# A two-layer graph kernel on one core: node passes one after the other, earlier stores of gathered rows, ten source-row buffers, and message arithmetic column by column on ScalarE

## The chip, the cores and the metric

The kernel runs on one core of a Trainium2 chip. The metric is device time in microseconds (us) of one execution; lower is better. The core has TensorE (PE: matmuls; PEld: its weight loads), VectorE (DVE), ScalarE (ACT), GpSimd (POOL), and SyncE (SP), which here only issues DMAs. POOL issues all indirect DMAs: gathers and scatters of one row for each of 128 partitions.

## The reference, cut to what matters

There are 100,000 nodes with 64 features, and 50,000 edges (src, dst), sorted by dst.

```python
h = relu(layernorm(x))
x = x + gcn(h)            # two GCN layers, 64 -> 128 -> 64, on all nodes
h = relu(layernorm(x))
x = x + l1(h)             # relation attention over the edges
# gcn layer: deg = count(dst) + 1; dinv = rsqrt(deg)
#   agg[dst] += h[src] * dinv[src] * dinv[dst];  out = agg + h * dinv^2 + b
# l1: att = sum(t_r * tanh(h_r + efeat)); a = softmax of att over the edges of one dst
#   h_nb[dst] += h[src] * a
#   out = leaky((h + h_nb) @ res_w1.T) + leaky(h * h_nb @ res_w2.T)
```

A node that is no destination has no sum over edges, so it needs only dense arithmetic. A destination is worked out again at its last edge, and its row is scattered over the dense result.

## The kernel before, in words

Nodes are held in NB = 49 blocks of 2048 (128 partitions x CB = 16 nodes). Edges are held as KE = 392 columns of 128; GE = 28 groups of GT = 14 columns. The program is written out by hand, engine by engine, with a semaphore for each hand-over. In order of time its stages are these.

- **Counting.** `hot(t)` makes two one-hot tiles in 16 bit for each of the 392 edge columns on VectorE: `lo_hot` (128 wide, L454) and `hi_hot` (784 wide, L455), four buffers each. TensorE multiplies them (L1534) and so adds up the degree of every node. Meanwhile POOL gathers x of each destination into `own` (5 buffers of a group); SP stores each group to the table `xd_t` in `keep_own`.
- **T pass** (`step_t`, 49 blocks): load x, layer norm and relu, store a row of 64 features plus a place and 1/sqrt(degree) to `node_rows`.
- **Q pass** (`step_q`, 49 blocks): load those rows and x, run the dense GCN (L1553, L1559, L1560, L1567), store `g1_t`; second layer norm, store `h_t`; residual products (L1575, L1583), store the output. `over_nodes` mixes the two passes: after step 5 one `step_q` follows every second `step_t`, on every engine, and the rest of `step_q` comes last. On SP, `own_after(turn)` says after which turn a gathered `own` group is stored: group g at turn 8 + 7g/4, none earlier.
- **E pass** (28 edge groups): once all T rows are stored, POOL gathers the rows of the sources into `near` (NBR = 6 buffers of a group, in the memory of the T pass); group g waits until VectorE has used group g - NBR (`S["d1"]`, L638). VectorE scales, runs a segmented scan (L641) and normalizes. It starts when all of the Q pass is stored.
- **D pass** (28 groups), the permutation by relation, the relation products and the softmax follow. The change touches there only the names of semaphores.
- **F pass** (28 groups, `step_f` on VectorE). For each group: message = neighbour row times weight (L912), scan (L916), sum of weights and its reciprocal (L920, L921), quotient into `fnb` (L922), the two operands of the product (L926, L927), then for the first segment of each partition mask, reduce and add (L929 to L931); then `f_post` of the group before (leaky L562, L900, and L902, which writes `fout`, two buffers, once the scatters of two groups before have landed). ScalarE copies between TensorE's banks (L1501, L1507) and spreads the mask (L1495). POOL scatters 14 columns of each finished group (L1196).

L1201 and L1196 are the helpers of all gathers and scatters, and L977 that of SP's DMAs, so their rows are told apart by the names of the tiles.

Of the kernel before, what the change touches and what calls it, by code (L numbers as in the profile page):

```python
# [5 lines left out]
ALU = mybir.AluOpType  # L6
ACT = mybir.ActivationFunctionType
AX = mybir.AxisListType
# [4 lines left out]
P = 128  # L13
# [48 lines left out]
NBR = 6  # L62
# [30 lines left out]
def build(nc, x, src, dst, eattr, etype, w1, b1, w2, b2, relw, rw1, rw2, out):  # L93
    with ExitStack() as ctx:
# [102 lines left out]
        near = part(arena, 0, [NBR, GT, TW])  # L197
# [4 lines left out]
        lo_hot = part(arena, Q0 + KN // 2, [4, P], F16)  # L202
        hi_hot = part(arena, Q0 + KN // 2 + 2 * P, [4, KN], F16)
        H0 = Q0 + KN // 2 + 2 * P + 2 * KN
# [35 lines left out]
        own = part(work, 0, [OWN, GW])  # L240
        W0 = OWN * GW
# [25 lines left out]
        fmask = part(work, 4 * FW, [DW * GT])  # L267
# [45 lines left out]
        lo_key, hi_key = m_idx[:].bitcast(F32), pos  # L313
        hot_made, hot_used = sem("one_hots_made"), sem("one_hots_used")
# [4 lines left out]
        Q = sems("q", "steps turned at h relu u g1 added x1 centered square var std hn hturned ht o os out")  # L319
# [8 lines left out]
        G = sems("d", "steps d1 mat run x1 centered square var std h")  # L328
# [10 lines left out]
        f = sems("f", "steps mat run two turned t o os half out")  # L339
# [39 lines left out]
        def _(dve):  # L379
# [26 lines left out]
            o.did(v.tensor_copy(lo_key[:], tmp_a[:, 0:KE].bitcast(I32)))  # L406
# [50 lines left out]
            for t in range(KE):  # L457
                hot(t)
# [38 lines left out]
            ot, oq = Steps(dve, T["steps"]), Steps(dve, Q["steps"])  # L497
# [40 lines left out]
            def q_centre(b):  # L538
# [5 lines left out]
                tt(cols(qxc), cols(x1), wide(st[:, 1, :], CB), ALU.subtract).then_inc(Q["centered"], 1)  # L544

            def q_variance(b):
                st = q_stat[:, b % 2]
                dve.wait_ge(Q["square"], b + 1)
                oq.do(v.tensor_reduce(st[:, 0, :], cols(qsq), AX.X, ALU.add))
                ts(st[:, 2, :], st[:, 0, :], 1.0 / D, EPS, ALU.mult, ALU.add).then_inc(Q["var"], 1)  # L550

            def q_h_rows(b):
                st = q_stat[:, b % 2]
                dve.wait_ge(Q["std"], b + 1)
# [1189 lines left out]
```

## Time and profile before

| what | value |
|---|---|
| time, median of 3 runs | 4637.77 us (4633.24 to 4641.26) |
| the profiled execution, its own time | 4642.34 us |
| its span, first to last instruction | 4640.6 us |
| busy | PE 34%, PEld 24%, DVE 54%, ACT 22%, POOL 65% |
| mean granted TensorE clock | 0.628 of full |
| HBM traffic | 265.55 MB read, 264.24 MB written, 114 GB/s |

No engine is busy for the whole span, and each stage has a limit of its own, so the shares are to be read stage by stage. A row of the timeline begins with the start and the duration; in brackets stands how long the engine had been idle and what released it.

### The profile page before, as it was taken

How to read it: one execution, taken by the hardware profiler on the slowest of the kernel's cores; microseconds unless marked ns; L12 is line 12 of the kernel's file. 1: busy time of each engine (PE TensorE's matmuls, PEld its weight loads, DVE VectorE, ACT ScalarE, POOL GpSimd, SP SyncE). 2: the span in 40 equal slices, each digit the busy share in tenths (PEclk: the TensorE clock that was granted, in tenths of full speed). 3: DMA queues.
4: the chain of work that ended last, by engine and by line, in shares of the span. 5: the costliest groups of instructions: out<-in, count | busy, mean ns of one | idle time of the engine just before them, and what ended most of it. 6: DMA issues, size and time to landing. Idle time of an engine off the chain costs nothing.

```text
span 4640.6 us, 31267 instructions
## 1 busy us (share of the span) xinstructions
PE 1563.3 (34%) x8094; PEld 1135.9 (24%) x8094; DVE 2526.9 (54%) x4033; ACT 1012.3 (22%) x1596; POOL 3032.0 (65%) x2761
## 2 busy tenths in 40 slices
PE   8835445688654340000000000023346600333331
PEld 2224334467543230000000000012335500322231
DVE  9967777777797666987741111112222200666663
ACT  0023333455432221111110000012222200222221
POOL 6026566640187776777757777777747777588887
PEclk9966666788776665555555555555556655666665
DMA  1056676776443334555532222234433300111110
GB/s 41 1 165 208 214 222 211 217 215 192 149 119 102 83 90 140 188 186 197 198 88 73 73 73 77 75 113 120 128 110 93 88 17 1 34 62 54 54 54 27
DMA packets 362638, 527.97 MB, mean 114 GB/s; under 512 B 220064, under 2 KB 232458, under 8 KB 362470
## 3 DMA queue, kind: packets, MB, share of 16 engines
q1 hardware_dynamic: 268166, 426.25, 28.2%
q0 software_dynamic: 94304, 99.74, 9.3%
q8 instruction: 74, 1.21, 0.1%
q14 instruction: 94, 0.77, 0.1%
HBM read 265.55 MB, written 264.24 MB: 114 GB/s over the span
## 4 chain that ended last, share of the span: by engine, by line
POOL 48%; issue 16%; PE 12%; DVE 11%; DMA 8%; ACT 2%; SPq 1%; POOLq 0%; DVEq 0%; ACTq 0%
POOL arena L1201 26%; POOL result L1196 10%; POOL slot_rows L1196 8%; DMA arena<-in_x 6%; POOL relf L1201 4%; PE banks L1534 3%; PE banks L1567 2%; PE banks L1669 2%; DMA work<-slot_rows 2%; PE banks L1559 1%; DVE arena L519 1%; SPq L977 1%; PE banks L1583 1%; DVE arena L455 1%; PE banks L1657 1%
## 5 line engine op out<-in xcount | busy, mean ns | idle before, releaser
L1201 POOL DMA_INDIRECT arena<-input_and_place_by_node,src_i x392 | 481.1, 1227 | 385.0 <-DVE arena L638 265.8
L1201 POOL DMA_INDIRECT work<-in_x,dsafe x392 | 414.1, 1056 | 435.6 <-DMA x_of_destination<-work 319.2
L1196 POOL DMA_INDIRECT result<-work,outi x392 | 502.1, 1281 | 164.3 <-issue 122.7
L1201 POOL DMA_INDIRECT arena<-g_by_node_and_edge,m_idx x392 | 445.1, 1136 | 121.1 <-issue 119.2
L1196 POOL DMA_INDIRECT slot_rows<-work,dsafe x392 | 404.3, 1031 | 141.7 <-issue 119.2
L1201 POOL DMA_INDIRECT arena<-h_by_node_and_edge,m_idx x392 | 405.3, 1034 | 119.5 <-issue 119.2
L1201 POOL DMA_INDIRECT relf<-slot_scores,src_i x392 | 369.9, 944 | 155.7 <-issue 128.5
L1657 PE MATMUL banks<-ident,work 128*128 128x128 f32 x456 | 111.5, 394 | 877.4 <-DMA work<-slot_rows 876.5
L819 DVE TENSOR_TENSOR work<-work,ends 128x896 f32<-128x896 f32 x28 | 46.7, 1668 | 568.1 <-DMA work<-h_by_node_and_edge 561.5
L1657 PEld LDWEIGHTS banks<-ident,work 128*128 128x128 f32 x456 | 80.3, 203 | 893.6 <-issue 696.0
L1669 PE MATMUL banks<-work 128*128 x912 | 209.6, 402 | 165.6 <-issue 115.1
L1567 PEld LDWEIGHTS banks<-w_sb,work 128*128 128x128 f32 x1568 | 224.4, 228 | 101.4 <-issue 101.4
L1567 PE MATMUL banks<-w_sb,work 128*128 128x64 f32 x1568 | 239.0, 316 | 0.0
L1669 PEld LDWEIGHTS banks<-work 128*128 128x128 f32 x912 | 180.0, 294 | 205.3 <-issue 205.3
L1699 PE MATMUL banks<-ident,work 128*128 128x128 f32 x392 | 90.5, 387 | 365.5 <-DVE work L927 365.5
L1553 PE MATMUL banks<-ident,arena 128*128 128x128 f32 x392 | 82.1, 347 | 388.3 <-DMA arena<-in_x 387.4
L1636 PE MATMUL banks<-last_run,carry 128*128 128x64 f32 (+1 forms) x6 | 1.8, 390 | 600.4 <-DVE last_run L775 593.2
L1534 PE MATMUL banks<-arena 128*128 128x392 f16 x784 | 195.6, 339 | 7.9 <-DVE arena L455 6.1
L833 DVE TENSOR_TENSOR dsti<-banks,work 128x256 f32<-128x256 f32 x57 | 24.2, 424 | 276.5 <-PE banks L1669 276.5
L1699 PEld LDWEIGHTS banks<-ident,work 128*128 128x128 f32 x392 | 72.2, 206 | 370.9 <-DVE work L927 370.9
L455 DVE TENSOR_SCALAR arena<-arena,pos 128x784 f16<-128x784 f16 x392 | 162.5, 415 | 0.0
L1553 PEld LDWEIGHTS banks<-ident,arena 128*128 128x128 f32 x392 | 59.7, 180 | 397.3 <-DMA arena<-in_x 341.6
(315 smaller groups left out, 5117.2 us busy)
## 6 DMA issues: line engine op xcount, KB each, us to landing
arena<-in_x SPq DMA_DIRECT2D x96, 512.0 KB, 5.3
slot_rows<-work SPq DMA_DIRECT2D x48, 912.0 KB
work<-slot_rows SPq DMA_DIRECT2D x114, 384.0 KB, 3.4
input_and_place_by_node<-arena SPq DMA_DIRECT2D x49, 528.0 KB, 2.9
arena<-input_and_place_by_node SPq DMA_DIRECT2D x49, 512.0 KB
g_by_node_and_edge<-arena SPq DMA_DIRECT2D x49, 512.0 KB, 3.3
h_by_node_and_edge<-arena SPq DMA_DIRECT2D x49, 512.0 KB, 3.1
arena<-x_of_destination SPq DMA_DIRECT2D x56, 448.0 KB, 4.3
```

The lines of the kernel that those rows point to most:

```text
L455: ts(hi_hot[:, t % 4, :], iota_h, hi_key[:, t:t + 1], None, ALU.is_equal).then_inc(hot_made, 1)
L519: stt(out=trows[:, b % 2, :, 0:D], in0=cols(tx[:, b % 3]), scalar=0.0, in1=wide(st[:, 4, :], CB), op0=ALU.max, op1=ALU.mult).then_inc(T["h ...
L819: oc.did(tt(by_column(pd1)[:, 0:GT, :], cols(phd), wide(ends[:, group(g)], GT), ALU.mult))
L977: sp.dma_start(to, of).then_inc(signal, 16)
L1196: pool.indirect_dma_start(out=table[:, :], out_offset=bass.IndirectOffsetOnAxis(ap=idx, axis=0), in_=of, in_offset=None, bounds_check=boun ...
L1201: pool.indirect_dma_start(out=to, out_offset=None, in_=table[:, :], in_offset=bass.IndirectOffsetOnAxis(ap=idx, axis=0)).then_inc(signal, 16)
L1534: ins = matmul(bank(4 + k)[:, 0:KE], lo_hot[:, t % 4, :], hi_hot[:, t % 4, k * KE:(k + 1) * KE], start=t == 0, stop=t == KE - 1, skip_grou ...
L1553: ins = transpose(bank(0)[:, k * P:(k + 1) * P], qh0[:, b % 3, half + k * P:half + (k + 1) * P], ident[:])
L1567: ins = matmul(bank(4 + n % 2)[:, k * D:(k + 1) * D], qhid[:, n % 2, at:at + P], w2_sb[:], start=True, stop=True)
L1657: ins = transpose(bank(j % 2)[:, k * P:(k + 1) * P], slot_w[:, j % SB, k, D:RW], ident[:])
L1669: ins = matmul(bank(2 + j % 4)[:, at], slot_ht[:, q, at], flat[:, w], start=True, stop=True)
L1699: ins = transpose(bank(c % 2)[:, k * P:(k + 1) * P], ftwo[:, at:at + P], ident[:])
```

## The change

Five things change; the D pass, the permutation, the relation products and the softmax keep their work.

- Counting: `lo_hot` is made for 14 columns by one `tensor_tensor` in 16 bit (128 x 1792), in two buffers; `hi_hot` stays one instruction for each column.
- The two node passes are no longer mixed: 50 turns of `step_t`, then 53 of `step_q`.
- SP stores `own` groups 0 to 11 (OWN_EARLY) before it does anything for the T pass beyond its first two loads. The other 16 are stored at turns 10, 13, 17, ... 62, each after the row store and the load of its turn.
- `near` has 10 buffers; the last four lie in the memory of `own`, so POOL waits before group 6 until every `own` group is stored.
- F pass: message, quotient and mask move from VectorE to ScalarE, as 14 activations each with a scale per partition; the sum over the mask is taken by 14 products with the identity on TensorE, added up in bank 7.

```diff
-NBR = 6
+OWN_EARLY = 12
+NBR = 10
-        near = part(arena, 0, [NBR, GT, TW])
+        near = [part(arena, k * GT * TW, [GT, TW]) for k in range(6)]
+        near += [part(work, k * GT * TW, [GT, TW]) for k in range(NBR - 6)]
             for b in range(NB + 1):
                 step_t(b)
-                if b >= 5 and b % 2:
-                    step_q((b - 5) // 2)
-            for k in range((NB - 5) // 2 + 1, NB + 4):
+            for k in range(NB + 4):
                 step_q(k)
...
-            def hot(t):
-                after(dve, hot_used, t - 3)
-                ts(lo_hot[:, t % 4, :], iota_h[:, 0:P], lo_key[:, t:t + 1], None, ALU.is_equal).then_inc(hot_made, 1)
-                ts(hi_hot[:, t % 4, :], iota_h, hi_key[:, t:t + 1], None, ALU.is_equal).then_inc(hot_made, 1)
+            for g in range(GE):
+                after(dve, hot_used, (g - 1) * GT)
+                tt(lo_hot[g % 2], iota_h[:, 0:P].unsqueeze(1).to_broadcast([P, GT, P]), wide(lo_half[:, group(g)], GT, P),
+                   ALU.is_equal).then_inc(lo_made, 1)
+                for t in range(g * GT, (g + 1) * GT):
+                    after(dve, hot_used, t - 3)
+                    ts(hi_hot[:, t % 4, :], iota_h, hi_key[:, t:t + 1], None, ALU.is_equal).then_inc(hi_made, 1)
...
# step_f on VectorE: leaves L912, L922, L929 to L931; f_post(g - 1) goes ahead of the two operands
-                    of.did(tt(by_column(fd1)[:, 1:SC, 0:D], cols(arena[:, g * GW:(g + 1) * GW]), wide(weights, GT), ALU.mult))
+                    dve.wait_ge(f["weighed"], g + 1)
-                    of.do(tt(cols(fnb), by_column(run)[:, 1:SC, 0:D], wide(st[:, 1, :], GT), ALU.mult))
+                if g > 0:
+                    f_post(g - 1)
+                if g < GE:
+                    dve.wait_ge(f["nb"], g + 1)
...
# SP
-                return [g for g in range(GE) if 8 + 7 * g // 4 == turn]
+                return [g for g in range(OWN_EARLY, GE) if 10 + 7 * (g - OWN_EARLY) // 2 == turn]
+            for g in range(OWN_EARLY):
+                keep_own(g)
             over_nodes(step_t, step_q)
# POOL, source rows
             for g in range(GE):
+                if g == 6:
+                    all_landed(pool, own_kept, OWN_KEPT)
                 after(pool, S["d1"], 2 * (g - NBR + 1))
...
# ScalarE
+            def f_weigh(g):
+                after(act, f["run"], g)
+                for k in range(GT):
+                    t = g * GT + k
+                    ins = activation(by_column(fd1)[:, 1 + k, 0:D], arena[:, t * D:(t + 1) * D], ACT.Copy, scale=weight[:, t:t + 1])
+                ins.then_inc(f["weighed"], 1)
+            def f_normal(g):
+                act.wait_ge(f["share"], g + 1)
+                after(act, f["two"], 2 * g)
+                for k in range(GT):
+                    ins = activation(cols(fnb)[:, k, :], by_column(frun[:, g % 2])[:, 1 + k, 0:D], ACT.Copy,
+                                     scale=estat[:, g % 2, 1, k:k + 1])
+                ins.then_inc(f["nb"], 1)
+            def f_masked(g):
+                after(act, f["summed"], g)
+                for k in range(GT):
+                    t = g * GT + k
+                    ins = activation(fmask[:, k, :], by_column(frun[:, g % 2])[:, 1 + k, :], ACT.Copy, scale=hm[:, t:t + 1])
+                ins.then_inc(f["masked"], 1)
             f_mat(0)
+            f_weigh(0)
             for g in range(GE):
+                f_normal(g)
                 if g + 1 < GE:
                     f_mat(g + 1)
+                    f_weigh(g + 1)
                 f_turned(g, 0)
                 for c in range(4):
                     if c < 3:
                         f_turned(g, c + 1)
+                    else:
+                        f_masked(g)
                     f_rows(g, c)
# TensorE, after the residual products of a group
+                pe.wait_ge(f["masked"], g + 1)
+                for k in range(GT):
+                    ins = matmul(bank(7)[:, 0:DW], ident[:], fmask[:, k, :], start=g == 0 and k == 0, stop=False,
+                                 skip_group_check=True)
+                ins.then_inc(f["summed"], 1)
```

## Rows read from the trace of the kernel before

**Rows 1.** Windows: busy time (x instructions) by engine, PE clock, DMA share, GB/s.

```profile
20.80:219.00 198.20, 195.56 (x784) 46.25 (x784) 197.40 (x785) 0.00 (x0) 57.22 (x59) 1.00 0.06 11
...
235.20:905.00 669.80, 326.16 (x1758) 249.08 (x1759) 507.06 (x705) 242.45 (x390) 370.05 (x344) 0.67 0.67 206
905.00:1250.50 345.50, 287.45 (x1772) 228.52 (x1770) 259.62 (x325) 183.69 (x296) 71.28 (x64) 0.84 0.63 196
```

**Rows 2.** Timeline of the counting: VectorE and TensorE's loads.

```profile
121.22 0.11 PEld L1534 LDWEIGHTS banks<-arena 128*128 128x128 f16 x2 [0.38 <-DVE arena L455]
...
121.26 0.41 DVE L455 TENSOR_SCALAR arena<-arena,pos 128x784 f16<-128x784 f16 x1
121.59 0.24 DVE L454 TENSOR_SCALAR arena<-arena,m_idx 128x128 f16<-128x128 f16 x1
```

**Rows 3.** Timeline of POOL: first and last of 70 own gathers of the counting.

```profile
5.68 1.17 POOL L1201 DMA_INDIRECT work<-in_x,dsafe  x1 [2.23 <-DVE dsafe L399]
...
94.76 0.94 POOL L1201 DMA_INDIRECT work<-in_x,dsafe  x1 [0.30 <-issue]
```

**Rows 4.** Timeline of the E pass: VectorE with two tensor inputs beside POOL's gathers.

```profile
1532.27 1.69 DVE L638 TENSOR_TENSOR arena<-arena 128x896 f32<-128x896 f32 x1 [6.43 <-DMA arena<-input_and_place_by_node,src_i]
1532.35 2.32 POOL L1201 DMA_INDIRECT arena<-input_and_place_by_node,src_i  x1 [0.30 <-issue]
```

**Rows 5.** Timeline: T pass with nothing beside it, then the first Q stores.

```profile
245.81 1.21 DVE L503 TENSOR_REDUCE t_stat<-arena 128x16 f32<-128x1024 f32 x1
...
251.25 1.21 DVE L503 TENSOR_REDUCE t_stat<-arena 128x16 f32<-128x1024 f32 x1
...
267.18 0.87 SPq L977 DMA_DIRECT2D arena<-input_and_place_by_node  x1
...
289.56 0.33 SPq L977 DMA_DIRECT2D g_by_node_and_edge<-arena  x1
```

**Rows 6.** Timeline, Q pass alone: SP's g1 stores, one a block; a start of TensorE.

```profile
928.88 0.32 SPq L977 DMA_DIRECT2D g_by_node_and_edge<-arena  x1
...
999.26 0.32 SPq L977 DMA_DIRECT2D g_by_node_and_edge<-arena  x1
...
1067.58 0.32 SPq L977 DMA_DIRECT2D g_by_node_and_edge<-arena  x1
...
1068.89 1.11 PE L1553 MATMUL banks<-ident,arena 128*128 128x128 f32 x4 [3.35 <-DMA arena<-in_x]
...
1084.73 0.32 SPq L977 DMA_DIRECT2D g_by_node_and_edge<-arena  x1
...
1095.99 0.32 SPq L977 DMA_DIRECT2D g_by_node_and_edge<-arena  x1
...
1200.37 0.34 SPq L977 DMA_DIRECT2D g_by_node_and_edge<-arena  x1
```

**Rows 7.** Windows of the source-row gathers alone: POOL busy (x gathers).

```profile
1261.30:1450.00 188.70, 154.52 (x113) 0.73 0.39 113
1450.00:1741.00 291.00, 231.58 (x196) 0.65 0.32 88
```

**Rows 8.** Timeline of the F pass: a scatter with VectorE idle, VectorE's wait.

```profile
4211.79 0.98 POOL L1196 DMA_INDIRECT result<-work,outi  x1 [0.30 <-issue]
...
4216.64 1.09 DVE L902 TENSOR_TENSOR work<-work 128x896 f32<-128x896 f32 x1 [8.73 <-DMA result<-work,outi]
...
4220.48 1.99 POOL L1196 DMA_INDIRECT result<-work,outi  x1 [0.30 <-issue]
```

**Rows 9.** Groups of instructions over the whole span: F pass, and ScalarE's sizes.

```profile
L1196 POOL DMA_INDIRECT result<-work,outi x392 | 502.1, 1281 | 164.3 <-issue 122.7 <-DVE work L902 41.6
L1349 ACT ACTIVATE arena<-arena 128x1024 f32<-128x1024 f32 x49 | 51.9, 1059 | 4.5 <-DVE arena L544 4.3
L1457 ACT COPY work<-work 128x896 f32<-128x896 f32 x28 | 47.6, 1700 | 185.1 <-DVE work L825 185.1
L1442 ACT ACTIVATE estat<-estat 128x14 f32<-128x14 f32 x28 | 6.0, 214 | 82.7 <-DVE estat L732 82.7
```

More of the change, by code:

```diff
@@ L201, in build @@
         iota_h = part(arena, Q0, [KN], F16)
-        lo_hot = part(arena, Q0 + KN // 2, [4, P], F16)
-        hi_hot = part(arena, Q0 + KN // 2 + 2 * P, [4, KN], F16)
-        H0 = Q0 + KN // 2 + 2 * P + 2 * KN
+        lo_hot = [part(arena, Q0 + KN // 2 + k * GT * P // 2, [GT, P], F16) for k in range(2)]
+        hi_hot = part(arena, Q0 + KN // 2 + GT * P, [4, KN], F16)
+        lo_half = part(arena, Q0 + KN // 2 + GT * P + 2 * KN, [KE], F16)
+        H0 = Q0 + KN // 2 + GT * P + 2 * KN + KE // 2
         iota_i = part(arena, H0, [KN], I32)
@@ L266, in build @@
         frun = part(work, 2 * FW, [2, FW])
-        fmask = part(work, 4 * FW, [DW * GT])
+        fmask = part(work, 4 * FW, [GT, DW])
         F0 = 4 * FW + DW * GT
@@ L338, in build @@
         soft = sem("softmax_steps")
-        f = sems("f", "steps mat run two turned t o os half out")
+        f = sems("f", "steps mat weighed run share nb two masked summed turned t o os half out")
         f_in, f_sent = ring("f_loaded"), ring("f_sent")
@@ L636, in step_e @@
                 dve.wait_ge(near_got[g % NBR], 16 * GT * (g // NBR + 1))
-                rows = near[:, g % NBR]
+                rows = near[g % NBR]
                 tt(by_column(ed1[:, q])[:, 1:SC, :], rows[:, :, 0:D], wide(rows[:, :, D + 1], GT), ALU.mult).then_inc(S["d1"], 1)
@@ L915, in step_f @@
                     dve.wait_ge(f["mat"], g + 1)
+                    dve.wait_ge(f["weighed"], g + 1)
+                    after(dve, f["masked"], g - 1)
                     v.tensor_tensor_scan(out=run, data0=fmat, data1=fd1, initial=0.0,
@@ L1023, in step_t @@
                     load_x(b + 2)
+                for g in own_after(b):
+                    keep_own(g)
             def load_q(b):
@@ L1220, in _ @@
                     t = g * GT + k
-                    gather(near[:, g % NBR, k, :], node_rows, src_i[:, t:t + 1], near_got[g % NBR])
+                    gather(near[g % NBR][:, k, :], node_rows, src_i[:, t:t + 1], near_got[g % NBR])
             all_landed(pool, e_a, EDGE_ROWS)
@@ L1406, in _ @@
                 act.wait_ge(near_got[g % NBR], 16 * GT * (g // NBR + 1))
-                copy(m_idx[:, group(g)], near[:, g % NBR, :, D]).then_inc(S["place"], 1)
+                copy(m_idx[:, group(g)], near[g % NBR][:, :, D]).then_inc(S["place"], 1)
                 if g + 1 < GE:
@@ L1437, in _ @@
                 st = estat[:, g % 2]
-                act.wait_ge(G["centered"], g + 1)
-                after(act, G["var"], g)
-                activation(dsq, dxc, ACT.Square).then_inc(G["square"], 1)
-                act.wait_ge(G["var"], g + 1)
-                activation(st[:, 3, :], st[:, 2, :], ACT.Sqrt).then_inc(G["std"], 1)
+                act.wait_ge(S["centered"], GE + g + 1)
+                after(act, S["var"], GE + g)
+                activation(dsq, dxc, ACT.Square).then_inc(S["square"], 1)
+                act.wait_ge(S["var"], GE + g + 1)
+                activation(st[:, 3, :], st[:, 2, :], ACT.Sqrt).then_inc(S["std"], 1)
             act.wait_ge(fix["ve"], at_step["fix variance"])
```

67 lines of the change are left out of this document (30 added, 37 removed).

## The prediction

> **What bounds the kernel now.** I read the page's 40 slices first: PE, ACT and DMA are high in different parts, so no single engine bounds the whole. Then I cut the span into stages with the windows [rows 1], and looked in each for what is waited for last (the chain, then the timeline).
>
> In the counting VectorE is busy for 197.4 of 198.2 us and TensorE's weight loads wait 0.38 us for it in each round [rows 1, 2], so VectorE sets the pace. A round takes 198.2/392 = 0.51 us; a narrow one-hot starts 0.33 after the wide one [rows 2], so the wide costs 0.33 and the narrow 0.17.
>
> In the node passes the DMA share is 0.67 and 0.63, VectorE is busy for 76% and 75%, and the PE clock is 0.67 and 0.84 [rows 1]. No engine is full; this is a loop through loads, TensorE and VectorE. Two pure paces can be read. T alone: 5.44 us a block [rows 5]. Q alone: 14.1 us a block with gathers beside it (5 intervals from 928.88 to 999.26), 13.4 without (15 intervals to 1200.37), and the mean hides two kinds, 11.3 and 17.2 us [rows 6]. In the long one TensorE had been idle 3.35 us for a load, and its four transposes take 1.11 us, 0.28 each [rows 6]; in the short one they take about half.
>
> In the E pass POOL made 113 gathers in its first 188.7 us and 196 in the last 291 [rows 7]: 23.4 us and then 20.8 us for a group of 14. VectorE lived on the six prefetched groups first: it used 6 + 113/14 = 14.1 groups in 188.7 us, 13.4 us each, and from then on waits 6.4 us a group for source rows [rows 4]. So POOL bounds it from 1450 on.
>
> In the F pass POOL scatters without a break; an undisturbed scatter takes 0.98 us and 0.30 of issue, VectorE waits 8.73 us a group for it [rows 8]. The mean of all is 1.281 us [rows 9], so a group costs 14 x 1.58 = 22.1 us, of which 4.2 are delays.
>
> **The delays of POOL.** A gather takes 2.32 us where VectorE's 1.69 us instruction with two tensor inputs is running [rows 4], 1.4 more than the 0.94 in [rows 3]; a scatter beside the scan takes 1.99 us, 1.0 more [rows 8]. Reduces and one-input instructions delay nothing here. The Trainium skill ("SBUF — State Buffer", Who interferes with whom) says the same: VectorE and GpSimd share a port pair, held for a whole instruction with two SBUF inputs. By that rule the new counting instruction speaks against the change. The trace has it for other instructions, not for this one.
>
> **The change, part by part.**
>
> *Counting.* Removed: 28 x 14 narrow one-hots, 2.4 us a group. Added: one instruction of 1792 elements a group. It isn't in the trace. L902 does 896 in 1.09 us [rows 8], so 1792 take 2.0 us at one a cycle; the wide one-hot does 784 in 0.33 [rows 2], so 0.75 us at its rate. I take 1.95, nearest to the row with two tensor inputs, and keep 0.8. The Trainium skill ("VectorE: DVE Perf Modes", Mode 2×_1P) gives two elements a cycle to 16-bit data only at step 1; one operand here is spread with step 0, which would leave 2.0 us. A group takes 14 x 0.33 + 1.95 = 6.6 us, 28 of them 185 us against 197: counting ends at 206, not 218.5. TensorE idles 1.9 us a group.
>
> But the T pass now waits for SP, which first stores 12 `own` groups, that is for POOL's 168th gather. From 5.68 at 1.29 us each [rows 3] that would be 222. Each new instruction of 1.95 us holds POOL up by 1.2 us (1.0 and 1.4 are the neighbours above). POOL makes 12 gathers before the counting, (185 - 28 x 1.2)/1.29 = 117 in it, and the 39 left take 50 us: 256. Landing 2 us, then the third block's x (4 us): its first reduce starts at 262 instead of 245.8 [rows 5]. **+16 us**, where VectorE alone would have given -12.
>
> *Node passes.* Third block at 262; 46 blocks at 5.44 are 250; the last row store 9.4 later; then the first Q load, after 22.4 us the first g1 store (267.18 to 289.56 [rows 5]). 3 us for 16 own stores between T's transfers: 547. T could slow down: in the mixed stage 49 T and about 25 Q blocks took 669.8 us, so at 13.6 for Q a T block cost at most 6.7; kept as the bound (+62 us), but the pure stretch has nothing to fight but 2 stores in 7 turns, so I take 5.44. Then 46 intervals to the store of block 46: gathers run beside about 17 of them (own groups to about 570, near 0 to 5 until 690, the rest after the last own store at turn 62, until 785): 17 x 14.1 + 29 x 13.4 = 628. From that store to the E pass 50.1 as before (1200.37 to 1250.5). End: 547 + 628 + 50 = 1225, against 1250.5. **-25 us** with the +16 in it. SP never waits long for an own group in this pass: they come every 18 to 20 us from 256 on, and are asked for every 19 us from turn 10 on.
>
> *Ten near buffers.* The four more are filled within the Q pass, POOL being idle there for 265 us before. So 18 groups are left instead of 22. VectorE at 13.4 a group and POOL at 23.4 meet after 10/(1/13.4 - 1/23.4) = 314 us; POOL has then made 13.4, the other 4.6 take 96 at 20.8: 410 us. With six buffers it was 188 + 291 = 479 [rows 7]. **-69 us**.
>
> *F pass.* VectorE loses two instructions of 1.67 us and three more; POOL was delayed 0.3 and 0.9 us by the two. But the order is tied to POOL: L902 waits for a scatter to land, then two products and the scan follow at once, and each catches a scatter. I expect 0.7 + 0.7 + 1.4 for these and 1.2 for the leaky pair: 4.0 instead of 4.2 to 4.4. 28 x 0.4 = 11 us less. The first group goes through two sets of activations: +4. **-7 us**; bounds: all delays but 3.2 gone (-30), random phase 4.8 (+15).
>
> ScalarE must stay under 22 us a group. One small activation: 14 elements take 0.214, 1024 take 1.059 [rows 9], so 0.2 fixed and 0.84 ns each; with a stride of 60 bytes 1.9 ns (1.70 us for 896 [rows 9]). 64 elements: 0.32 alone, 0.17 if the fixed part overlaps the next. 42 of them: 7 to 13.4 us; I take 12, since the scale per partition was not seen. With the mask spread 0.95 and eight copies 3.5: 16.5, and some 3 of waits for TensorE. Under 22, so hidden. The Trainium skill ("ScalarE: Activation LUTs", What ACT_TABLE_LOAD costs) adds 93 ns for a pointer operand and takes 93 off back to back; by it 42 cost about 12.3 us, and the sum stays. TensorE's 14 products (0.3 each) fall where it waits.
>
> *The rest.* Stages from the D pass to the softmax keep their length. Sum: -25 - 69 - 7 = -101. The profiled execution has 4640.6 of span and 1.7 around it, 4642.3; less 101 is 4541. The median of the runs shown is 4.5 lower: **4537**.
>
> **Rivals.**
>
> 1. *POOL is not held up in the counting* (the new instruction is short or leaves gaps). Then T's third block starts at 233: 29 less, 4508. For: narrow instructions delay nothing now. Against: [rows 4]. Chance 0.18.
> 2. *Q runs at its short kind throughout*, 11.3 us: 48 x 2.3 = 110 less, 4427. For: 11.3 exists [rows 6]. Against: gathers beside it, 14.1. Chance 0.10.
> 3. *Q runs at its long kind*, 17.2: 48 x 3.6 = 173 more, 4710, slower than before. It decides from 13.6 + 101/48 = 15.7 us a block on. TensorE would go into each block after an idle stretch and at 1.2 GHz; a mean of 13.6 is 39% of such blocks. For: loads and stores now stand closer. Against: both stretches read here, 20 blocks, average 14.1 or less. Chance 0.06.
> 4. *ScalarE bounds F*: an activation of 0.4 us makes 16.8 + 4.5 + 3 = 24.3 a group: 28 x 2.3 = 64 more, 4601. Chance 0.10.
> 5. *TensorE's clock falls in the counting's gaps* of 1.9 us. A round then costs 0.65, two products of 392 columns at 1.2 GHz: 256 us, third block at 304, 42 more: 4579. Against: TensorE already waits in each round [rows 2] at clock 1.00 [rows 1], and a gap of 1.9 is shorter than the 3.35 of [rows 6]. Chance 0.07.
>
> The forecast has 0.49, its own range 4495 to 4590 (Q at 13.1 to 14.4: -25 to +35; T at up to 6; F -22 to +15).
>
> **How the numbers follow.** 4450 to 4610 takes in the forecast and rivals 1, 4 and 5, and leaves out 2 and 3, 0.16. Faster by more than 0.2% (some 9 us, about what a measurement here can tell): all but rival 3 and a mixture of the bad ones, 0.91; same 0.02; slower 0.07.
>
> **What would show it.** Gathers into `own` beside the new instruction over 2 us long, and the third block near 262. T at 5.4 to 5.6. g1 stores 13 to 14 us apart. 84 gathers, a pause, 56 gathers within Q; the E pass some 69 us shorter, VectorE waiting only in its last third. F: 22 us a group, POOL without idle time, ScalarE near 17 us busy. Wrong if Q's pace leaves 13 to 14.4, or if F's groups are longer than 23 us.

## The result and the profile after

| kernel | time, median of 4 runs | lowest to highest |
|---|---|---|
| before | 4635.51 us | 4629.84 to 4641.26 |
| changed | 4495.43 us | 4484.93 to 4499.22 |

The ratio is 0.9694, 95% interval 0.9672 to 0.9716: faster by 140 us, where 100 were forecast. On the chips of the experiments below some executions take 160 to 220 us longer than the others of the same kernel; the times given there are medians of all executions, the ratios and comparisons leave the long ones out.

The two profiled executions have spans of 4640.6 and 4497.4 us, 143.2 less. The first record of each stage tells where the 143.2 us come from:

| stretch | change of its length | forecast |
|---|---|---|
| start of the program to the first load of the E pass | -60.2 us (1250.5 to 1190.3) | -25 |
| E pass, to the first gather of the D pass | -71.0 us | -69 |
| D pass to the last score gather | +8.7 us | 0 |
| from there to the first scatter of the F pass | +5.4 us | +4 |
| F pass, first to last scatter | -26.3 us | -11 |

The first row holds two things. The first row store of the T pass comes 20.9 us later (265.49 instead of 244.59), and from there to the first load of the E pass it takes 924.8 us instead of 1005.9, 81 less. Before, a turn of two T blocks and one Q block took 27.2 us (20 intervals of the g1 stores from 309.41 to 852.64); the paces of the separate passes, 5.43 and 12.80, make 23.7 of it. 23 mixed turns at 3.5 us are some 80 us. This is read from the stages; no run tests it by itself where they are undisturbed.

Windows of the changed kernel, counting, T pass, and Q pass with and without source-row gathers (busy time of PE, PEld, DVE, ACT, POOL with instructions, PE clock, DMA share, GB/s):

```profile
20.80:207.00 186.20, 135.90 (x773) 51.64 (x774) 184.40 (x416) 0.00 (x0) 151.76 (x114) 1.00 0.17 41
207.00:530.00 323.00, 2.96 (x19) 1.30 (x17) 277.44 (x418) 63.22 (x99) 249.92 (x240) 0.51 0.67 205
530.00:800.00 270.00, 228.79 (x1415) 175.23 (x1415) 193.22 (x247) 147.76 (x234) 183.60 (x170) 0.85 0.77 220
800.00:1170.00 370.00, 317.30 (x2069) 252.35 (x2069) 301.69 (x381) 214.35 (x345) 0.00 (x0) 0.89 0.65 202
```

The counting takes 186.2 us instead of 198.2 [rows 1], VectorE is as full as before, and TensorE's clock stays at 1.00, its upper level of 2.4 GHz, although TensorE now idles in every group. Timeline of the counting, VectorE, POOL and TensorE:

```profile
102.72 2.01 DVE L455 TENSOR_TENSOR arena<-arena 128x1792 f16<-128x1792 f16 x1
...
101.91 1.03 POOL L1200 DMA_INDIRECT work<-in_x,dsafe  x1 [0.30 <-issue]
103.25 2.29 POOL L1200 DMA_INDIRECT work<-in_x,dsafe  x1 [0.31 <-issue]
...
105.21 4.00 PE L1566 MATMUL banks<-arena 128*128 128x392 f16 x23 [1.78 <-DVE arena L459]
```

The new instruction takes 2.01 us, the pace of L902 in [rows 8] and not that of the wide one-hot. The own gather beside it takes 2.29 us, 1.35 more than the last of [rows 3]. The others take 1.03; before, they took 0.94 and 1.01 in turn. The cost shows at SP, whose rows come next:

```profile
210.05 54.92 SPq L975 DMA_DIRECT2D x_of_destination<-work  x4
...
265.49 0.67 SPq L975 DMA_DIRECT2D input_and_place_by_node<-arena  x1
...
274.63 0.32 SPq L975 DMA_DIRECT2D input_and_place_by_node<-arena  x1
...
280.06 0.32 SPq L975 DMA_DIRECT2D input_and_place_by_node<-arena  x1
```

SP is in its own stores until 265. VectorE had been idle since its first two blocks, waiting for the x that SP loads after these stores, as its first reduce of the third block shows:

```profile
270.33 1.22 DVE L504 TENSOR_REDUCE t_stat<-arena 128x16 f32<-128x1024 f32 x1 [34.17 <-DMA arena<-in_x]
```

That is 24.5 us later than before [rows 5]. Then the pace is 5.43 us a block to the last row store at 528 (262.5 us for the 49 stores). SP's g1 stores of the Q pass (first, an interval of each kind, last):

```profile
550.88 0.33 SPq L975 DMA_DIRECT2D g_by_node_and_edge<-arena  x1
...
903.54 0.32 SPq L975 DMA_DIRECT2D g_by_node_and_edge<-arena  x1
914.80 0.32 SPq L975 DMA_DIRECT2D g_by_node_and_edge<-arena  x1
...
1061.90 0.32 SPq L975 DMA_DIRECT2D g_by_node_and_edge<-arena  x1
1078.14 0.32 SPq L975 DMA_DIRECT2D g_by_node_and_edge<-arena  x1
...
1165.18 0.32 SPq L975 DMA_DIRECT2D g_by_node_and_edge<-arena  x1
```

48 intervals in 614.3 us are 12.80 each. The two kinds of [rows 6] are still there: 30 intervals average 11.24 us and 18 average 15.39. The first four intervals take 41.4 us together (7.6, 9.5, 13.1 and 11.3). From 592.25 to 759.29, with source-row gathers beside for most of the time, 12 intervals average 13.9; the 32 after that average 12.7. In the pass TensorE waits for x 66.0 us (groups of instructions, 545 to 1190):

```profile
L1585 PE MATMUL banks<-ident,arena 128*128 128x128 f32 x380 | 66.7, 304 | 66.1 <-DMA arena<-in_x 66.0
```

The F pass, timeline of ScalarE's three sets of 14, then of POOL and VectorE:

```profile
4206.23 4.21 ACT L1531 ACTIVATE work<-work,hm 128x65 f32<-128x65 f32 x14
...
4210.60 4.22 ACT L1522 ACTIVATE work<-work,estat 128x64 f32<-128x64 f32 x14
...
4215.55 3.52 ACT L1515 ACTIVATE work<-arena,tmp_a 128x64 f32<-128x64 f32 x14
...
4211.41 2.20 POOL L1195 DMA_INDIRECT result<-work,outi  x1 [0.30 <-issue]
...
4217.78 1.64 POOL L1195 DMA_INDIRECT result<-work,outi  x1 [0.30 <-issue]
4219.72 1.70 POOL L1195 DMA_INDIRECT result<-work,outi  x1 [0.30 <-issue]
4221.73 2.06 POOL L1195 DMA_INDIRECT result<-work,outi  x1 [0.31 <-issue]
```

The 42 activations take 11.95 us. Of the 14 scatters of this group four are longer than 0.98: one beside the leaky pair, two beside the products, one beside the scan. What was waited for in the pass (engine, waited for, us in total, times, longest):

```profile
DVE work L563 <- ACT work L1508: 231.6, 27, 12.5
...
DVE work L902 <- DMA result<-work,outi: 73.8, 21, 4.9
POOL result L1195 <- DVE work L902: 48.3, 7, 46.4
```

VectorE waits more for ScalarE (8.6 us a group) than for the scatters (before, 197.4 us for these in all), but POOL waits only 1.9 us in all after its first group, and its scatters fell from 1281 ns [rows 9] to 1214.

### The profile page after: what moved, and what is told of

Its sections match the earlier page's. It is cut to its first block, busy times and chain, and to the rows that moved or that the text cites. A ratio compares the mean times of both kernels' runs of the same rounds, so it can differ in the third digit from the quotient of the medians.

```text
span 4497.4 us, 33923 instructions
## 1 busy us (share of the span) xinstructions
PE 1617.4 (36%) x8878; PEld 1264.9 (28%) x8878; DVE 2353.9 (52%) x3528; ACT 1341.4 (30%) x2772; POOL 3041.0 (68%) x2761
## 4 chain that ended last, share of the span: by engine, by line
POOL 47%; issue 17%; DVE 16%; PE 8%; DMA 7%; ACT 4%; SPq 1%; POOLq 0%; DVEq 0%; ACTq 0%
POOL arena L1200 21%; POOL slot_rows L1195 8%; POOL result L1195 8%; POOL work L1200 6%; POOL relf L1200 4%; DMA arena<-in_x 4%; DMA work<-slot_rows 2%; PE banks L1701 2%; PE banks L1599 1%; DVE arena L520 1%; DVE arena L506 1%; DVE t_stat L504 1%; DVE t_stat L511 1%; DVE arena L536 1%; DVE work L563 1%
## 5 line engine op out<-in xcount | busy, mean ns | idle before, releaser
L1200 POOL DMA_INDIRECT arena<-input_and_place_by_node,src_i x252 | 313.9, 1246 | 482.9 <-DVE arena L639 406.4
L1195 POOL DMA_INDIRECT result<-work,outi x392 | 475.8, 1214 | 169.8 <-issue 121.5
L1200 POOL DMA_INDIRECT work<-in_x,dsafe x392 | 442.5, 1129 | 121.7 <-issue 119.4
L1689 PE MATMUL banks<-ident,work 128*128 128x128 f32 x456 | 114.0, 400 | 891.2 <-DMA work<-slot_rows 890.8
L1689 PEld LDWEIGHTS banks<-ident,work 128*128 128x128 f32 x456 | 82.3, 207 | 907.6 <-issue 696.1
L563 DVE SCALAR_TENSOR_TENSOR work<-work 128x1024 f32<-128x1024 f32 (+1 forms) x77 | 116.8, 1516 | 323.1 <-ACT work L1508 240.2
L1200 POOL DMA_INDIRECT work<-input_and_place_by_node,src_i x140 | 173.0, 1236 | 71.8 <-issue 71.5
L1751 PE MATMUL banks<-work,ident 128*128 128x65 f32 x784 | 170.2, 412 | 118.8 <-ACT work L1531 118.8
L1751 PEld LDWEIGHTS banks<-work,ident 128*128 128x128 f32 x784 | 164.9, 324 | 124.1 <-ACT work L1531 124.1
L1429 ACT COPY arena<-arena 128x896 f32<-128x896 f32 x28 | 47.8, 1708 | 406.9 <-DMA arena<-g_by_node_and_edge,m_idx 406.9
```

The costliest lines, as they stand in the source:

```text
L563: return stt(out=to, in0=of, scalar=0.01, in1=of, op0=ALU.mult, op1=ALU.max)
L1195: pool.indirect_dma_start(out=table[:, :], out_offset=bass.IndirectOffsetOnAxis(ap=idx, axis=0), in_=of, in_offset=None, bounds_check=boun ...
L1200: pool.indirect_dma_start(out=to, out_offset=None, in_=table[:, :], in_offset=bass.IndirectOffsetOnAxis(ap=idx, axis=0)).then_inc(signal, 16)
L1429: copy(by_column(ed1[:, g % 2])[:, 1:SC, :], sum2[:, g % SUM2]).then_inc(G["d1"], 1)
L1689: ins = transpose(bank(j % 2)[:, k * P:(k + 1) * P], slot_w[:, j % SB, k, D:RW], ident[:])
L1751: ins = matmul(bank(7)[:, 0:DW], ident[:], fmask[:, k, :], start=g == 0 and k == 0, stop=False, skip_group_check=True)
```

## The experiments

They ran on three chips on which the kernel before takes 5222.78, 5218.31 and 5222.06 us, not 4636. The changed kernel itself was run only on the third of them. Ratios are to the kernel before on the same chip, and stages are compared by their first and last records. There is no trace of the kernel before on these chips, so its stages there are not known.

### What the slower chips change

`after2`, the changed kernel again. 

> The changed kernel as it is, as a base for the kernels beside it. On the two chips used so far for experiments the kernel before took 5218 and 5223 us instead of 4636, and the stages that the change does not touch were longer there too, with engines idle for 5 to 60 us at a time and nothing in the profile that they wait for. Theory A (that is a slow supply of instructions, and it takes about as much from both kernels outside the counting): where the kernel before takes 5220 us this one takes 5010 to 5050, ratio 0.960 to 0.968. Theory B (the changed kernel, with 33923 instructions instead of 31267, suffers more): 5100 us or more, ratio above 0.977. Where the kernel before takes 4636 us again: 0.967 to 0.972.

5092.55 us, ratio 0.9736 (0.9708 to 0.9764): the gain here is 138 us in a longer time. It lies between the two theories. The E pass (first to last store of its input, 411.1 us where the result was measured) has 413.4 here and the F pass 599.3 against 598.1, but the permutation pass has 1198 instead of 1041 and the scores with the softmax 778 instead of 552. The T pass (first to last row store) takes 322.1 us instead of 262.5, with eight turns in a row of 11.2 us where 5.43 is the pace. In these turns POOL gathers as fast as on the chip of the result, and VectorE and ScalarE do half (windows of the changed kernel, of the result and then here):

```profile
300.00:380.00 80.00, 0.00 (x0) 0.00 (x0) 78.00 (x119) 19.09 (x30) 62.16 (x59) 0.50 0.78 243
```

```profile
300.00:380.00 80.00, 0.00 (x0) 0.00 (x0) 37.09 (x56) 9.54 (x15) 62.50 (x58) 0.50 0.43 122
```

The first Q blocks stall as well. Windows of the changed kernel here, and below it of the same with NBR = 6:

```profile
588.00:700.00 112.00, 19.31 (x84) 12.97 (x84) 4.04 (x6) 6.74 (x9) 84.88 (x90) 0.55 0.31 66
700.00:875.00 175.00, 141.64 (x880) 111.36 (x880) 126.32 (x162) 94.63 (x151) 3.85 (x5) 0.82 0.62 192
875.00:960.00 85.00, 35.84 (x138) 26.41 (x139) 19.84 (x25) 13.91 (x23) 52.75 (x54) 0.54 0.33 84
```

```profile
580.00:700.00 120.00, 22.96 (x83) 15.55 (x84) 1.44 (x3) 6.27 (x8) 86.01 (x91) 0.51 0.29 59
700.00:875.00 175.00, 142.52 (x977) 110.35 (x976) 140.47 (x180) 103.58 (x167) 0.00 (x0) 0.92 0.68 212
875.00:960.00 85.00, 73.23 (x504) 58.10 (x504) 71.98 (x92) 52.02 (x85) 0.00 (x0) 0.94 0.71 217
```

Where POOL gathers back to back (the first window of each, the third of the first kernel), TensorE does about 0.7 to 1.6 matmuls a us; where POOL is idle it does 5 to 6. On the chip of the result the same Q pass beside gathers ran 5.2 (x1415 in 270 us). The idle time in these stretches is put down to "issue" or to "remote" for the most part, not to a wait of the program.

`narrow`, wide low one-hots replaced by the narrow ones, 14 a group.

```diff
-                tt(lo_hot[g % 2], iota_h..., wide(lo_half[:, group(g)], GT, P), ALU.is_equal).then_inc(lo_made, 1)
+                    ts(lo_hot[g % 2][:, t % GT, :], iota_h[:, 0:P], lo_key[:, t:t + 1], None, ALU.is_equal).then_inc(lo_made, 1)
```

> The changed kernel with the low one-hots of the counting built per column again (seven short instructions of VectorE a group, as in the kernel before); all else as changed. Theory A (the own gathers beside the wide instruction take 2.29 us instead of 1.03, so SyncE, which waits for each of them, comes late to the node rows): the own gathers take about 1.0 us, the own stores end near 225 us into the execution instead of 265, the first row store stands near 240 instead of 265, and the kernel is 15 to 25 us faster than the changed one: ratio to the kernel before about 0.965 where the changed one has 0.969. Theory B (SyncE's own stores cost what they cost, about 1.2 us each, and the own gathers are no limit): the first row store stays within 5 us of 265 and the ratio at 0.969 or above, since counting itself ends some 12 us later.

5294.36 us, 1.0138 (1.0119 to 1.0157). Neither theory: the counting itself became slow. Timeline:

```profile
99.36 0.25 DVE L456 TENSOR_SCALAR arena<-arena,m_idx 128x128 f16<-128x128 f16 x1 [5.03 <-remote]
99.53 0.42 DVE L457 TENSOR_SCALAR arena<-arena,pos 128x784 f16<-128x784 f16 x1
104.95 0.37 DVE L456 TENSOR_SCALAR arena<-arena,m_idx 128x128 f16<-128x128 f16 x1 [5.00 <-remote]
105.12 0.42 DVE L457 TENSOR_SCALAR arena<-arena,pos 128x784 f16<-128x784 f16 x1
```

A pair of one-hots every 5.6 us instead of 0.51 while POOL gathers every 1.25 us; the first row store stands at 527.7 us. The own gathers do take 0.94 us here, but VectorE is idle beside most of them, so that settles nothing; SP's lateness is tested by `best` below.

`sep_only`, the kernel before with the two node passes one after the other and nothing else.

```diff
-                if b >= 5 and b % 2:
-                    step_q((b - 5) // 2)
-            for k in range((NB - 5) // 2 + 1, NB + 4):
+            for k in range(NB + 4):
                 step_q(k)
```

> The kernel before with one part of the change alone: the T pass over all blocks, then the Q pass; own groups are still stored at turn 8 + 7g/4, near has 6 buffers. Theory A (the passes gain only together with the earlier stores): turns of 5.44 us ask for an own group every 9.5 us, POOL makes one every 18.5, so SP, and with it the T pass, waits for gathers; T ends near 632 us instead of 505, the E pass starts near 1320 instead of 1250, ratio to before about 1.015. Theory B (separate passes gain by themselves): T keeps 5.44 us a block, E pass starts near 1180, ratio about 0.985.

5328.42 us, 1.0194 (1.0162 to 1.0225). By its stages, the mechanism of theory A is there: the T pass, from first to last row store, takes 399.3 us, and 268.1 and 267.7 in the next two runs, which have the earlier stores. These 131 us are close to the 127 expected (632 against 505). After the first 20 blocks SP waits for an own group ahead of every second row store:

```profile
485.20 0.32 SPq L975 DMA_DIRECT2D x_of_destination<-work  x1
...
504.31 0.32 SPq L975 DMA_DIRECT2D x_of_destination<-work  x1
```

So the separate passes need the earlier stores. The counting, with narrow one-hots, is slow here only while POOL makes its 70 gathers (first window), and then runs at its normal pace:

```profile
21.00:95.00 74.00, 16.56 (x48) 4.23 (x48) 13.73 (x48) 0.00 (x0) 55.29 (x59) 0.58 0.14 26
95.00:285.00 190.00, 181.90 (x732) 42.61 (x732) 182.04 (x734) 0.00 (x0) 0.00 (x0) 0.97 0.00 1
```

`sep_early`, the same with OWN_EARLY = 12 too. 

> The kernel before with separate passes and the earlier stores of own groups (12 before the T pass, then every 3.5 turns), the narrow one-hots, the old F pass and 6 near buffers kept. Theory A: without the long two-input instruction POOL has its 168 gathers done near 222 us, so the third block's first reduce stays near 246 us; T ends near 505, Q at 13.0 us a block, E pass starts near 1182: 68 us less, ratio 0.985. Theory B (Q at 13.6 as forecast): E pass near 1210, ratio 0.991.

5336.69 us, 1.0218 (1.019 to 1.0245), a clear miss. Run again beside the changed kernel as `sep_early2`. 

> Once more the kernel before with the separate passes and own stores in the counting alone (narrow one-hots, six buffers, old last pass), where its first run was disturbed. Theory A (the order is worth about 25 us, the forecast): where the kernel before takes 4636 us, ratio 0.993 to 0.996. Theory B (the order is worth all that the changed kernel gained ahead of the edge pass, 60 us): 0.985 to 0.988. Where it takes 5220 us, counting again lasts to about 500 us, since VectorE's short instructions come late there, and the ratio is 1.02.

5340.72 us, 1.0219 (1.02 to 1.0238). In `sep_early2` too the first row store waits until 526 us for the counting, while the E pass (479.4 and 481.9 us) and the F pass (624.3 and 624.9) are as long as in the kernel before on the chip of the result (481.4 and 624.4). With the earlier stores POOL gathers through the whole counting, and the counting in short instructions lasts until 501 us instead of 286 in `sep_only`. So whether the separate order gains by itself can't be read here, and what it is worth where the counting isn't disturbed was not measured.

### Own stores and loads

`early8`, OWN_EARLY = 8 in the changed kernel, the other groups stored from turn 2 on instead of 10. 

> The changed kernel with 8 instead of 12 groups of own rows stored ahead of the node pass and the other 48 spread over its turns. Theory A (the node pass starts late only because SyncE works through the own stores first): the first row store comes 25 to 35 us earlier, at 230 to 240 us, where VectorE's counting is the bound, the pace of 5.4 us a block holds, and the kernel is about 25 us faster than the changed one: ratio 0.964. Theory B (the own stores and gathers that are moved into the turns lengthen the turns by as much): the node pass starts earlier but its pace is above 5.6 us a block, and the ratio stays at 0.969.

5066.59 us, 0.966 (0.9617 to 0.9703), where the changed kernel has 0.9736, on another chip. In its profiled execution, of 5218.63 us, the counting lasts until 404 us, so the stages can't be read there. The same edit stands in `best`, where the timeline of VectorE and SP shows the third block's first reduce at 234.98, with no idle time ahead of it:

```profile
234.98 1.21 DVE L504 TENSOR_REDUCE t_stat<-arena 128x16 f32<-128x1024 f32 x1
...
239.20 0.32 SPq L975 DMA_DIRECT2D input_and_place_by_node<-arena  x1
...
240.04 0.80 SPq L975 DMA_DIRECT2D x_of_destination<-work  x1
...
244.63 0.32 SPq L975 DMA_DIRECT2D input_and_place_by_node<-arena  x1
```

The first row store is at 233.8 us, 265.7 in the changed kernel on that chip, so 32 us earlier, and 5.43 us pass between the two row stores shown, with an own store in the turn. The first ten turns keep this pace; then come ten of 9.8 us, as there are eight of 11.2 in `after2`, and the whole pass takes 311.9 us against 322.1. Theory A.

`qload`, SP's load of block k+3 right behind the g1 store of block k.

```diff
-                if k + 2 < NB:
-                    load_q(k + 2)
+                    load_q(2)
...
                     load(node_block(g1_t, k), qg1[:, k % 2], q_g1[k % 2])
+                if k + 3 < NB:
+                    load_q(k + 3)
```

> The changed kernel with SyncE's load of block k+3 issued right behind the store of block k instead of ahead of that of block k+1; nothing else. Theory A (the pace of 12.8 us a block in the second node pass comes from loads that land late: TensorE waits for them 66 us in 31 places, and its clock is at 0.85 to 0.89 because of such waits): the waits for loads nearly vanish, the pace falls to 11.3 to 11.8 us and the kernel is 45 to 70 us faster than the changed one: ratio 0.955 to 0.959. Theory B (the pace is set by the chain of VectorE, ScalarE and TensorE through the running maxima, with VectorE waiting 78 us for ScalarE's L1341): the waits for loads shrink, the pace stays at 12.5 to 12.8, and the ratio at 0.966 to 0.969.

4990.27 and 5020.61 us: two executions, too few for an interval. Repeated as `qload2` beside the changed kernel. 

> Once more the changed kernel with SyncE's load of block k+3 issued right behind the store of block k, now beside the changed kernel itself. Theory A (late loads set the pace of the second node pass): from the first load to the last store of that pass 40 to 60 us less than in the changed kernel on the same chip. Theory B (they do not): within 10 us of it.

5018.96 us, 0.9574 (0.9545 to 0.9603), where the changed kernel has 0.9736 (0.9708 to 0.9764): the intervals don't touch. Q pass from its first load to its last output store: 745.5 us instead of 806.6. That stage alone would prove little, since its stalls beside the gathers vary: with the old load it takes 806.6, 798.3 and 787.1 (`after2`, `f_old`, `mask_dve`), with the new one 715.5, 745.5 and 786.3 (`qload`, `qload2`, `best`). The pace away from the gathers is the better measure. The same window without gathers, first of the changed kernel on that chip, then with the earlier load:

```profile
960.00:1212.00 252.00, 220.47 (x1472) 173.63 (x1470) 208.41 (x264) 151.85 (x246) 0.00 (x0) 0.91 0.68 211
```

```profile
960.00:1212.00 252.00, 225.06 (x1569) 179.41 (x1568) 225.13 (x286) 160.76 (x263) 0.00 (x0) 0.95 0.76 229
```

7% more matmuls in the same time, DMA share 0.76 instead of 0.68. The g1 stores are now all of the short kind: 46 of 48 intervals average 11.4 us, none is between 12.6 and 20, and two hold the stalls. Waits for x no longer stand among the waits of that window; in the changed kernel they are 24.7 us there. Theory A.

`best`, both edits. 

> Both edits together: the load of block k+3 right behind the store of block k, and 8 instead of 12 groups of own rows stored ahead of the node pass. Theory A for both (SyncE is late at the first row store because of the own stores; late loads set the second pass's pace): first row store at 230 to 240 us instead of 265 and the second pass 40 to 60 us shorter, in all 65 to 95 us less than the changed kernel where no instructions are late. Theory B (own stores cost the same in the turns, and the pass is set by its chain): within 10 us of the changed kernel.

5007.59 us, 0.9588 (0.9572 to 0.9605): 77 us less than the changed kernel, as theory A had it, but no less than `qload2` alone, so the earlier start adds nothing to the total here. Its 32 us are in the trace (its profiled execution took 5035.52), and the Q pass then stalls longer beside the gathers, in three intervals of 68 to 77 us: 786.3 us to the last output store instead of 745.5. It is the best version together with `qload2`; what it takes where those stalls are absent was not measured.

### Ten buffers

`nbr6`, the changed kernel with NBR = 6, and without the wait for the own groups before group 6. 

> The changed kernel with 6 instead of 10 near buffers. Theory A: the E pass is bound by POOL once the prefetched groups are used; it gets 71 us longer, ratio to before 0.985. Theory B (part of the shorter E pass comes from elsewhere, such as less contention): less than 40 us, ratio under 0.978.

5086.21 us, 0.9735 (0.9708 to 0.9762), the ratio of the changed kernel itself. By the total, the four buffers are worth nothing here. By stages they are worth nearly what was forecast: the E pass (first to last store) takes 478.2 us with six and 413.4 with ten (`after2`), 65 us less where 71 were expected. All nine kernels with ten are between 411.1 and 414.4, and five with six, the kernel before among them, between 478.2 and 481.9. What they gain there they lose in the Q pass (first load to last output store 806.6 us with ten, 736.6 with six): its gathers of groups 6 to 9 run beside blocks 14 to 17, and in the windows above that is the stall from 875 to 960 us, which the kernel with six doesn't have. Two intervals of the g1 stores take 86 us there in `after2`, where 23 would be usual; `f_old` and `mask_dve` have the same (87 and 85). On the chip of the result gathers slow Q far less (13.9 against 12.7 us a block).

### The last pass

`f_old`, the changed kernel with the F pass of before. 

> The changed kernel with the F pass of before (message, quotient and mask on VectorE). Theory A: POOL's scatters are held up 4.4 us a group instead of 3.1, so a group takes 22.4 us instead of 21.4 and the F pass gets 26 us longer, less 5 us for the shorter start: ratio to before 0.974. Theory B (ScalarE is by now the limit of the F pass and the move gained nothing): within 8 us, ratio under 0.9715.

5100.18 us, 0.9766 (0.9743 to 0.9789). F pass, first to last scatter: 624.8 us, against 599.3 in `after2` and 624.4 in the kernel before. The new pass is worth 25 us, in agreement with the 26.3 above. Theory A.

`mask_dve`, the mask, its sum and the addition on VectorE again, messages on ScalarE.

```diff
-                    f_masked(g)
+                    of.do(tt(masked, run.rearrange(...)[:, :, 1:SC], over_features(hm[:, group(g)], DW), ALU.mult))
+                    of.do(v.tensor_reduce(hs1[:], masked, AX.X, ALU.add))
+                    of.do(tt(hsum[:], hsum[:], hs1[:], ALU.add))
```

> The changed kernel with the masked product, its reduction and its sum in the last pass on VectorE again, as in the kernel before; the messages stay by column on ScalarE, without the 14 columns of the mask (4.2 us a group). Theory A (in the changed last pass, at 21.4 us a group, ScalarE is nearly the bound: VectorE waits 8.4 us a group for its messages): ScalarE falls to about 11 us a group, VectorE rises to about 16 and the pace stays between 21 and 21.5 us since GpSimd's gathers and scatters, 20.4 us, set it: within 5 us of the changed kernel, ratio 0.968 to 0.970. Theory B (the chain gather, ScalarE's messages, VectorE's run and scatter sets the pace, and 5 us more of VectorE in it lengthens it): 1 to 3 us a group, 28 to 84 us slower than the changed kernel, ratio 0.975 to 0.987.

5076.48 and 5084.37 us: two executions, so it is read by its trace. F pass 606.3 us, 7.0 more than with the mask on ScalarE. Scatters by groups of instructions, with `mask_dve` first and `after2` below:

```profile
L1199 POOL DMA_INDIRECT result<-work,outi x392 | 484.0, 1235 | 171.2 <-issue 122.4 <-DVE work L903 48.8
```

```profile
L1195 POOL DMA_INDIRECT result<-work,outi x392 | 477.1, 1217 | 173.1 <-issue 123.0 <-DVE work L902 50.1
```

392 x 18 ns are the 7 us: POOL sets the pace in both, and the masked product costs what it delays POOL by. ScalarE relieved of 4.2 us a group gains nothing. Theory A on what binds, a little over its size.

## Why the prediction was right

The median of 4495.43 lies 42 below the forecast of 4537, within 4450 to 4610, but at the bottom edge of the forecast's own range (4495 to 4590). The prediction also named a sign by which its mechanism would be wrong, Q's pace outside 13 to 14.4 us, and that sign came: 12.80. Two terms gave too small a gain, Q by 37 us and F by 14; losses elsewhere hid some of it: 4 at the first g1 store and 9 between the D pass and the last score gather. By the steps of the prediction:

- **Counting, right, a little small.** 1.95 us was taken for the new instruction, 2.01 measured; the extra for the gather beside it 1.2, measured 1.35. Third block at 262, measured 270.33. The other own gathers took 1.03 us there and not 0.94 and 1.01 in turn, so POOL made 114 in the counting and not 117, and the 168th starts at 262.15 where it was to be done by 256. (That one-input instructions "delay nothing" was read too simply: before, every second gather beside the one-hots was 0.07 longer.) That SP's order ties this to the node pass is shown by `best`: four own groups fewer ahead of it, 32 us earlier.
- **T pass, right.** 5.44 us a block taken, 5.43 measured; the bound of 6.7 wasn't needed. First g1 store 547, measured 550.88: the 8 us lost at the third block, less some 4 that its allowances held.
- **Q pass, the term that was mis-sized.** 628 us were taken for 46 intervals, 13.6 each; they measured 591.1, 37 less. 15 of the 37 lie in the first four intervals, priced at 14.1 each: they took 41.4 us and not 56.4, with the loads of three blocks issued ahead of the first store. The later part with gathers was right (14.1, measured 13.9). The part without was taken from 15 intervals [rows 6] that average 13.4, and measured 12.7 over 32: 20 us. The short kind was as expected (11.24) and the share of long ones too (18 of 48, before 9 of 23), but a long one averages 15.4 instead of 16.5. Why they are shorter stays open; in the earlier 15 intervals the clock was 0.84 [rows 1] over a stretch that also held gathers, here it is 0.89.
- **Rival 2**, the short kind throughout, was given 0.10 and didn't happen. `qload2` shows that it needs only the loads of a block issued 3 us earlier (1.4 us behind the g1 store instead of 4.6): the long kind comes from loads that land late. So the two kinds were a symptom of SP's order, and that could have been read: TensorE waited for `in_x` ahead of the long block.
- **Ten buffers, right**: -69 forecast, -71.0 measured; 6 against 10 buffers in otherwise equal kernels 65.
- **F pass, right in kind, small in size.** -7 us was taken, with a range of -22 to +15; -26.3 and +5.4 make -21 measured. A group was to have 4.0 us of delays; (1214 - 982) x 14 = 3.2 are left of 4.2. The leaky pair (1.22) and the products (0.66 and 0.72) are as taken; the scan delays 1.08 instead of 1.4, and not every group has all four. The first group costs 5.4 instead of 4. ScalarE: 12 us for the 42 taken, 11.95 measured; 16.5 in all taken, 434.7/28 = 15.5 measured. Rival 4 falls with it. The 12.3 us that the prediction gave beside its 12 can't be worked out again from the two figures named there, which cancel; nothing rests on it.
- **Rivals 1, 3 and 5 fall.** POOL is held up; Q's mean is below its own, not above; the clock is 1.00 in the counting.
- **The rest was not unchanged.** 8.7 us were lost between the D pass and the last score gather, 6.3 of them between the first score gather and the store of the second half of the scores (253.2 us instead of 246.9 with the same instructions); POOL waits 7.66 us for that store ahead of its 197th gather, 0.96 before. Why the scores came later is not explained.

The Trainium skill's rule on the shared port ("SBUF — State Buffer", Who interferes with whom) now has its row for this instruction too: 2.01 us of VectorE with two inputs, a gather of 2.29 beside it. And its rule on step 1 ("VectorE: DVE Perf Modes", Mode 2×_1P) agrees: 1792 elements of 16 bit, one operand spread, took 2.01 us, as against 0.75 at the rate of the one-hot of 784. No run has the same instruction with both operands at step 1, so that the step is the reason isn't shown here.

## What to carry to other kernels

When intervals of a loop fall into two kinds, look for what is late ahead of the long kind before averaging them: here loads issued 3 us sooner made nearly all of them short, worth 1.6% by themselves. Time saved on one engine is only gained if no queue that works in order has more to do first: with 12 own groups ahead of the row stores, the 12 us saved on VectorE ended in a T pass that started 24.5 us later; with 8 (`best`) its third block starts at 235, 11 us before the 246 of the kernel before. And where the same program can meet different chips, compare stages, not totals: four buffers gained 65 us in one stage and lost as much in another.

## What the runs showed of the hardware

On three chips the kernel before took 5220 us instead of 4636, and the changed one, on one of them, 5092 instead of 4495. All traces there are longer in the same stages and hardly at all in others (for the changed kernel E 413 against 411, F 599 against 598, but scores and softmax 778 against 552). In the gaps every compute engine but POOL sits idle, and for the most part no row names a wait of the program. They come where POOL gathers back to back: 5.6 us for a pair of one-hots, 85 us for 138 matmuls that take some 25 elsewhere, 11.2 us for a T block. `sep_only` shows that the gathers are a condition: the same instructions of the counting run at 0.65 a us on VectorE while POOL gathers and at 3.9 once it has stopped.

A slow supply of instructions that competes with the gathers, theory A of `after2`, would look like this, but the DMA queues speak against it. The packets that carry instructions have queues of their own (q8 and q14). The queues of `narrow` from 40 to 200 us, where a pair of one-hots takes a steady 5.6 us, and then from 340 to 500 us, at the normal pace:

```profile
q0 software_dynamic: 4099, 4.20, 15.0%
q1 hardware_dynamic: 1296, 4.13, 6.8%
```

```profile
q8 instruction: 6, 0.10, 0.3%
q14 instruction: 5, 0.04, 0.1%
```

In the slow stretch no packet of instructions moves at all, so TensorE and VectorE work through instructions that were there already, one pair for every four or five gathers. What each of them waits for stays open, and no run changed it by itself. The number of instructions doesn't sort the stages: the F pass, beside back-to-back scatters, runs 9.6 instructions a us (PE, PEld, DVE, ACT and POOL together) undisturbed, and the T pass stalls though it has 2.6. POOL's own pace may matter as well: on the chip of the result it made 0.71 to 0.77 gathers or scatters a us in the T pass, the Q pass beside gathers, the permutation and the scores, all of which are longer on the other chips, and 0.60 to 0.69 in the counting and the E, D and F passes, which are not. No run tests that either.

The practical side is measured, with one exception. There the 28 wide one-hots in place of 392 narrow ones let the counting run at its normal pace (`after2`: VectorE x416 in 186 us, as on the first chip), while `narrow` took until 527 us to the first row store; its ratio is 1.0138 against 0.9736, more than 190 us, though it was put at 12. But the profiled execution of `early8`, with wide one-hots too, has the slow counting: POOL makes 79 gathers from 100 to 200 us there and VectorE 21 instructions. So the wide instruction makes it rarer and doesn't rule it out. Whether it helps because the instructions are fewer or because it holds up POOL (0.61 gathers a us instead of 0.80) isn't separated.
